# Two-layer attention and expert kernel: the two turns of an expert block's rows, side by side or on either side of the next block's first product

## What is computed

```python
xn = _layernorm(x)
x = x + linear_attention0(xn) + moe0(xn)      # 32 experts, 8 per token, inner width 176, and a shared expert
xn = _layernorm(x)
x = x + gated_linear_attention1(xn) + moe1(xn)  # 8 experts, 2 per token, and a shared expert
```

```python
h = jax.nn.silu(x @ wg.T) * (x @ wu.T)
acc = acc + cw[:, None] * (h @ wd.T)
```

## Time and profile before

| | us |
|---|---|
| median of 3 runs | 1150.62 (1150.17 to 1154.53) |
| span of the profiled execution | 1312.9 |
| PE busy in it | 1068.4 (81%) |
| ACT busy | 384.0 (29%) |
| DVE busy | 538.7 (41%) |
| POOL busy | 316.8 (24%) |
| block loop, first to last row turn | 379.1 to 888.8 |

### The profile page before, as it was taken

How to read it: one execution, slowest core, us unless ns; L and a number is a source line. 1 busy time by engine, 2 the same in 40 slices (tenths; PEclk the granted TensorE clock), 3 DMA queues, 4 the chain that set the end, 5 groups by cost and what they waited for, 6 DMA issues and landing times.

```text
span 1312.9 us, 17206 instructions
## 1 busy us (share of the span) xinstructions
PE 1068.4 (81%) x4648; PEld 760.6 (58%) x4648; DVE 538.7 (41%) x1355; ACT 384.0 (29%) x963; POOL 316.8 (24%) x327
## 2 busy tenths in 40 slices
PE   5935302678749999999999999998488998999996
PEld 4713201344526666677677666665356776888774
DVE  6512100276402322233244444345478548444443
ACT  2200000111113333333333333442124433434521
POOL 3267777000000000000133331205556110000112
PEclk9867656788769999999999999998879999999999
DMA  9992222000065555555577777354332011001001
GB/s 369 422 379 102 96 96 96 16 0 0 6 265 174 172 174 172 172 176 175 174 227 226 227 226 215 100 158 137 105 96 78 31 32 35 28 27 36 25 17 48
DMA packets 100189, 174.37 MB, mean 133 GB/s; under 512 B 13782, under 2 KB 64946, under 8 KB 99458
## 3 DMA queue, kind: packets, MB, share of 16 engines
q1 hardware_dynamic: 87810, 139.69, 32.2%
q0 software_dynamic: 12288, 33.57, 8.1%
HBM read 104.52 MB, written 68.68 MB: 132 GB/s over the span
## 4 chain that ended last, share of the span: by engine, by line
PE 64%; another core or an unknown queue 12%; issue 10%; DVE 5%; DMA 4%; ACT 2%; POOL 1%; SPq 1%; POOLq 0%; DVEq 0%; ACTq 0%
PE banks L812 16%; PE banks L833 12%; PE banks L860 5%; PE banks L862 5%; PE banks L861 5%; DMA xb<-xg 4%; PE banks L796 3%; PE banks L823 3%; PE banks L733 2%; PE banks L1028 1%; PE banks L786 1%; PE banks L692 1%; PE banks L667 1%; PE banks L741 1%
## 5 line engine op out<-in xcount | busy, mean ns | idle before, releaser
L812 PE MATMUL banks<-wgu,xt 128*128 x760 | 299.6, 477 | 1.4 <-issue 0.8
L542 POOL DMA_INDIRECT yk<-yg,slot_idx x128 | 124.3, 971 | 596.8 <-DMA yg<-yb 449.5
L833 PE MATMUL banks<-wd,ht 88*128 88x256 f32 x760 | 197.2, 381 | 6.4 <-DVE ht L1609 6.4
L1609 DVE COPY ht<-banks 88x256 f32<-88x256 f32 x190 | 80.0, 421 | 217.8 <-PE banks L823 197.1
L531 POOL DMA_INDIRECT xg<-tok,slot_idx x128 | 125.3, 979 | 82.4 <-issue 51.1
L833 PEld LDWEIGHTS banks<-wd,ht 88*128 88x128 f32 x760 | 129.8, 191 | 18.3 <-DVE ht L1609 7.9
L812 PEld LDWEIGHTS banks<-wgu,xt 128*128 128x128 f32 x760 | 120.2, 193 | 34.2 <-issue 24.1
L1187 ACT ACTIVATE sg<-banks 128x176 f32<-128x176 f32 x190 | 60.2, 317 | 209.8 <-PE banks L812 177.0
L692 PE MATMUL banks<-shd,sh_t 128*128 128x256 f32 x96 | 32.4, 487 | 108.3 <-ACT sh_t L1119 56.9
L1616 DVE TENSOR_TENSOR hid<-sg,banks 128x176 f32<-128x176 f32 x190 | 64.2, 338 | 124.0 <-ACT sg L1187 120.8
L860 PE MATMUL banks<-xn_hi,w_gu_hi 128*128 128x512 f32 x224 | 102.9, 459 | 0.7 <-DVE gate L1840 0.7
(11 more groups left out here) (254 smaller groups left out, 1527.4 us busy)
## 6 DMA issues: line engine op xcount, KB each, us to landing
wd<-in_wdn SPq DMA_DIRECT2D x190, 176.0 KB
xg<-zeros SPq DMA_DIRECT2D x38, 640.0 KB, 17.4
xb<-xg SPq DMA_DIRECT2D x190, 128.0 KB
yg<-yb SPq DMA_DIRECT2D x190, 128.0 KB
w_raw<-in_moe SPq DMA_DIRECT2D x28, 384.0 KB
wgu<-in_wgu SPq DMA_DIRECT2D x1, 4576.0 KB
wgu<-in_wgu SPq DMA_DIRECT2D x2, 2112.0 KB, 12.7
wgu<-in_wgu SPq DMA_DIRECT2D x1, 2464.0 KB, 13.4
```

The costliest lines, as they stand in the source:

```text
L542: pool.indirect_dma_start(yk[:, n % YK_RING, :], None, yg[h], bass.IndirectOffsetOnAxis(ap=slot_idx[:, t, k:k + 1], axis=0))\
L812: mm = pe.matmul(bank[2 + g % 2][:, 0:2 * F0], xt[:, g % 2, k, :], wgu[:, bass.ds(expert[0], 1), k, :].rearrange("p a n -> p (a n)"), star ...
L833: mm = pe.matmul(bank[7][:, 0:D], ht[:, g % 2, c, :], wd[:, g % WD_RING, c, :], start=c == 0, stop=c == 1, skip_group_check=True)
L1609: v.tensor_copy(ht[:, g % 2].rearrange("p c n -> p (c n)"), bank[6][0:FH, 0:D])\
```

## The change

The two transposes of a block's rows no longer stand next to each other. In iteration g, the first of block g+2 (with both waits, `xb_in` and `xt_done`) stands at the head, before the up product of block g+1 and so before the table read for it; the second (which raises `x_tp`) stays where both were, after the second half of the up product and before the down product. The first two blocks, ahead of the loop, are turned as before. No instruction is added or removed; no other engine's program changes.

```diff
-            def block_turn(g):
-                pe.wait_ge(xb_in[g % XB_RING], 16 * (g // XB_RING + 1))
-                if g >= 1:
-                    pe.wait_ge(xt_done, g)
-                for k in range(KD):
-                    mm = pe.transpose(bank[4][:, k * P:(k + 1) * P],
-                                      xb[:, g % XB_RING, k * P:(k + 1) * P], eye)
-                mm.then_inc(x_tp, 1)
+            def block_turn(g, k):
+                if k == 0:
+                    pe.wait_ge(xb_in[g % XB_RING], 16 * (g // XB_RING + 1))
+                    if g >= 1:
+                        pe.wait_ge(xt_done, g)
+                mm = pe.transpose(bank[4][:, k * P:(k + 1) * P], xb[:, g % XB_RING, k * P:(k + 1) * P], eye)
+                if k == 1:
+                    mm.then_inc(x_tp, 1)
...
             for g in range(ALL_BLOCKS):
+                if g + 2 < ALL_BLOCKS:
+                    block_turn(g + 2, 0)
                 if g + 1 < ALL_BLOCKS:
                     block_up(g + 1, 0)
                 block_hidden_turn(g)
                 if g + 1 < ALL_BLOCKS:
                     block_up(g + 1, 1)
                 if g + 2 < ALL_BLOCKS:
-                    block_turn(g + 2)
+                    block_turn(g + 2, 1)
                 prepare(0, g - PREP0_AT, 0, bank[5])
                 block_down(g)
```

More of the change, by code:

```diff
@@ L1056, in unit_down @@
                 mm.then_inc(down_mm, 1)
-            block_turn(0)
-            block_turn(1)
+            for g in range(2):
+                block_turn(g, 0)
+                block_turn(g, 1)
             block_up(0, 0)
```

## The result

| | before | after |
|---|---|---|
| median, us | 1150.53 (4 runs, 1150.17 to 1154.53) | 1287.37 (4 runs, 1283.31 to 1289.99) |
| ratio | | 1.1162, 95% interval 1.1125 to 1.1198 |
| span of the profiled execution | 1312.9 | 1287.6 |

The two spans must not be subtracted: by them the change would be a gain of 25 us. The span after agrees with its median; that of before was 162 us above it. It shows where the first one had been long. The row turns of L796 bound the loop; first the changed kernel, then the unchanged one again (count, duration min/median/max in ns, first to last start in us).

What follows compares the result with a forecast made beforehand. PE's own stream was taken to bound the expert loop. Copy 0.79, read chain 0.90 and products 1.51 make 3.20 us a block, 0.71 more; over 182 blocks that adds 129 us to 1150.6, giving 1280, range 1205 to 1335.

Steps and rivals of the forecast that it cites:

- PE's stream bounds the loop, and a gap costs its full length: Expert loop: PE busy 243.22 of 244.00 us, 2.57 us a block, so any gap on PE costs its full length.
- The copy to `xt` ends 0.79 us after the second turn's start: ACT's copy of turned rows: still ends 0.79 us after the up product's end; the earlier signal gains nothing.
- The read starts with the end of that copy and not of the `ht` copy: PE's sequencer: the table read stands behind the first turn's `xt_done` wait, so starts some 0.75 us later in the block.
- The chain, 0.90 us: PE's sequencer: from the releasing copy's end through the table read to the up product's weight load, 0.90 to 1.12 us.
- From the weight load to the next turn, 1.51 us: PE: from the up product's weight load to that product's end, 1.51 us with no further wait.
- The sum: One block: 0.79 + 0.90 + 1.51 = 3.20 us, 0.71 more than before; over 182 blocks, 129 us.
- The row loads, 1.4 us in the sum and 15 as a bound: First turn's `xb_in`, needed 1.4 us earlier: 1.4 us lost once, at most 15 us over 11 waits.
- The `ht` cover: Down product reached 0.11 us sooner after the hidden turn, nothing to spare for the `ht` copy: 0 to 0.03 us a block.
- Rival A: The `xt_done` wait sits with the transpose and lets the sequencer pass to the read: 1150.6 us, within 1 us; 6%.
- Rival B: The read's chain is shorter outside the profile: 1198 us at half length, 1240 at three quarters; 18%, centred on 1240.
- Rival C: Gaps in PE's stream also make its clock fall part of the time: 96 us on top, 1376 us; 12%.

Runs made afterwards that it cites:

- wait_only: Unchanged kernel, both row turns side by side, with one more wait for `xt_done` at the head of each iteration, ahead of the table read: 1266.0 us, ratio 1.100.
- two_banks: Changed kernel with odd blocks' rows turned in PSUM bank 0, so the first turn waits for the copy of the block before last: 1213.6 us, ratio 1.052.
- behind_up: Changed kernel with the first turn moved from the head to between up half 0 and the hidden turn: 1171.7 us, ratio 1.016.
- two_banks_loads: As two_banks, with each row load issued one iteration earlier: 1165.0 us, ratio 1.010.

## Why the prediction was right

The forecast was 1280 us in a range of 1205 to 1335; 1287.4 was measured.

- **PE's stream bounds the loop, and a gap costs its full length.** Held. The rest of the span is the same within 5 us in every run.
- **The copy to `xt` ends 0.79 us after the second turn's start.** Held: from 602.87 in the timeline after, the next copy starts at 603.28 and takes 0.37, 0.78 us. The signal that comes earlier relative to the up product bought nothing, since the copy starts 0.21 or 0.22 us after silu in every timeline here.
- **The read starts with the end of that copy and not of the `ht` copy.** Held: 0.16 us behind it, 600.35 to 600.5. A wait for that copy put on the read itself costs 115 us (wait_only).
- **The chain, 0.90 us.** This term was too small: 1.01 us in the block at 600, since a wait instruction and the transpose stand between the copy and the read. The prediction named that step, 0.10 us, but only in the upper bound. wait_only shows the chain without it, 0.93 in the block shown.
- **From the weight load to the next turn, 1.51 us.** Held to the digit: 601.36 to 602.87.
- **The sum.** 0.78 + 1.01 + 1.51 = 3.30 us a block instead of 3.20. The mean in mid-loop grew from 2.54 to 3.33, by 0.79 where 0.71 was forecast. 188 x 0.79 = 149; the loop grew by 138.4. The missing 10 us are mostly blocks in which another stop already stood: nine blocks near the end of the loop, where the layer-1 transposes are, grow by 0.11 us at most. The prediction had taken off 6 blocks for them. The two errors, a term too small by 0.08 and a count too large, are of opposite sign, and the total came out 8 us low, 129 against 137.
- **The row loads, 1.4 us in the sum and 15 as a bound.** Right for this change, where the longer block gave them time. They became a cost of 49 us only in two_banks, when the other wait had been taken away: the next to be late.
- **The `ht` cover.** The 0.08 us are there (45.9 us of waits at the weight loads of the down product), but in the changed kernel they lie beside the longer wait. They count where that one is gone, in behind_up and two_banks_loads.
- **Rival A** (the wait does not hold up the read): refuted. The changed kernel's wait for `xt_done` is an instruction of the sequencer and so no test of a wait that sits with the transpose, which is how the prediction put this rival; the wait for the rows in two_banks is one, and the read stood behind it until 503.3. The Trainium skill, "Perfetto Trace Analysis", section "Tensor Engine Instruction (MATMUL, LD_WEIGHTS)", has the sequencer free for the next instruction once a matrix instruction is in the wait queue; for a table read as the next instruction two_banks shows otherwise.
- **Rival B** (a shorter chain without the recording): refuted. All four runs of the changed kernel took 1283 us or more, and the first profile was longer than the second by 141 us ahead of the loop and 17 behind it, but only 8 in it.
- **Rival C** (the clock): refuted; 1.00 from 300 to 800 us, with PE busy for 85% and idle in pieces of about half a microsecond in nearly every block. The Trainium skill, "TensorE: Matmul & The Clock Gate", section "A second HAM failure mode: psum-queue depth-cycling", lets frequent short idles make the clock oscillate; that is not borne out here.

## What to carry to other kernels

A wait in an engine's program has to be placed by what stands behind it, not by when the waiting instruction is needed: a transpose that the array could take late without harm held back a table read whose register chain was not covered. Scalar reads and register operations belong ahead of waits that can be late, and as soon as the queue in front of them is free; here moving the read alone made the kernel 0.8% faster. When one late wait is removed, look at once for the semaphore of the same instruction that comes next, as the row loads did.

## What the runs showed of the hardware

- A `TENSOR_LOAD` on PE's sequencer does not overtake a product or transpose that waits in front of it: it began within 0.2 us of the release, by the `ht` copy (601.48 to 601.5), by the `xt` copy (600.35 to 600.5) or by a DMA (503.3). It doesn't wait for the array: at 601.5 the down product in front of it had not begun (601.67).
- The read, its register operations and the assertion take 0.64 us up to the next sequencer step, and 0.85 to the weight load that uses the register (600.51 to 601.36). Read a second time, they cost 0.646 us more a block.
- A row load of 128 KB took 2.6 us from issue to landing in the block shown of two_banks, and 2.7 us in the median of its loop (2.4 to 4.1). With over half of the loss removed there, it was this load that held the read.
